# Bias of similarities in a cross-attention kernel: from six small TensorE passes to one VectorE multiply-and-sum with a broadcast load

## The chip, the cores and the metric

One Trainium2 chip, one core of it. The metric is the device time of one execution in microseconds (us); the kernel before takes 112.34 us, the median of three runs (112.3 to 112.38).

## What is computed

A block of three parts acts on x, 128 rows of 256 (L = 128, D = 256): a cross attention to a context of S = 12544 rows of 256, a self attention and a feed-forward part. The change touches the first one alone. Cut to what matters (h is x after layer normalisation, c the context):

```
w1, w2, w3 = w_sim[:d], w_sim[d:2*d], w_sim[2*d:]
Sim = (h @ w1)[:, :, None] + (c @ w2)[:, None, :] + einsum('bid,bjd->bij', h * w3, c) + b_sim[0]
A = softmax(Sim, axis=2)
hq_hat = A @ c
Batt = softmax(max(Sim, axis=2), axis=1)
hc_bar = Batt @ h
feats = concatenate([h, hq_hat, h * hq_hat, h * hc_bar])
x = x + feats @ W_qv + b_qv
```

The term h @ w1 + b_sim is one number for each of the 128 rows. It falls out of A, which a shift of a whole row does not change, and is needed only for Batt, that is for the row maximum of Sim. The kernel calls it hw1.

## The kernel before, in words

The context is cut into 25 chunks of 512 rows, 0 to 24; the last has 256. It is read twice from DRAM: transposed as "keys", for the scores, and as "rows", for the sum weighted by A. Every chunk of either kind is one load of 512 KB into one of ten slots of the ring `raw`. Both kinds go through one queue, SyncE's (SP): x first, then the keys 0 to 24, then the rows 0 to 24. `wait_for_slot` holds an item until the item ten places before it has been used. Into the keys two loads of 512 KB of the weights are mixed, behind keys 12 and 18 (`W_BEHIND`). The small vector `vec` and the scalar `bias` are loaded by ScalarE's queue at the start.

Phase of keys. TensorE multiplies a chunk in one of two ways. The "native" chunks 0, 4, 8, 16 and 24 are multiplied as they are (L925). The others are split into a high and a low part: ScalarE copies the high part (`keys_high`, L488), VectorE subtracts it from the chunk to get the low part (`keys_low`, L698), and TensorE does three products, L940 and L944 on the high part and L954 on the low. In chunks 10, 12, 14, 18, 20 and 22 (`SHARED`) GpSimd takes 448 of the 1024 columns of the low part (L454), so VectorE's piece has 576. For every two chunks VectorE empties two PSUM banks into `neg_scores` and takes the running minimum of the negated scores in `neg_max` (`running_max`, L721). VectorE's order is written out by hand: behind chunk k goes the low part of k + 2, and behind every odd k the running maximum of the pair. ScalarE also sums and centres weight blocks between its copies (L528, L539), the first four of them from the load behind key 12 and the next four from that behind key 18.

Turn of the phases. TensorE transposes the exponentials of chunks 0 and 1 (`turn`, L968), does the last native chunk between them, and multiplies them with their rows (`mix_early`, L979). `mix_early(0)` waits until the maximum of chunks 22 and 23 has been taken, because it writes into a PSUM bank that held scores:

```
                if k == 0:
                    pe.wait_ge(max_done, eviction_of[22] + 2)
```

Phase of rows. For chunks 2 to 24 TensorE transposes the exponentials of chunk k + 2 (L968) and does the products of chunk k (`mix`, L997 and L999). VectorE makes the low parts of rows and of transposed exponentials (L698, L728), ScalarE and GpSimd the high parts.

hw1 before. Behind the scores of chunk 1 TensorE does two products of `normed_t` with a column of `vec` (L1045) and one of a row of ones with `bias` (L1047) into column 0 of `mixed_ps`. A product of 32-bit numbers at full precision is several passes in the profile, so these are six rows of the trace. At the turn VectorE subtracts the last `neg_max` from it into `sim_max` (L766). Since `mix` overwrites `mixed_ps`, TensorE waits for `sim_max_done` ahead of the phase of rows. In chunk 3 `sim_max` is spread over the columns (L1060), and Batt follows from it.

## Time and profile before

| | |
|---|---|
| time, median of 3 runs | 112.34 us (112.3 to 112.38) |
| the profiled execution's own time | 112.1 us |
| its span, first to last instruction | 110.3 us |
| granted TensorE clock | 1.0 over the whole span |
| busy: TensorE, VectorE, ScalarE, GpSimd | 95%, 84%, 75%, 27% |
| moved by DMA | 29.82 MB |

The span leaves out 1.8 us of the execution's time that lie around it. A busy share is an average over phases: it does not say which engine holds the others at a given place. The rows that do follow further down.

### The profile page before, as it was taken

How to read it: one execution, taken by the hardware profiler on the slowest of the kernel's cores; microseconds unless marked ns; L12 is line 12 of the kernel's file. 1: busy time of each engine (PE TensorE's matmuls, PEld its weight loads, DVE VectorE, ACT ScalarE, POOL GpSimd, SP SyncE). 2: the span in 40 equal slices, each digit the busy share in tenths (PEclk: the TensorE clock that was granted, in tenths of full speed). 3: DMA queues.
4: the chain of work that ended last, by engine and by line, in shares of the span. 5: the costliest groups of instructions: out<-in, count | busy, mean ns of one | idle time of the engine just before them, and what ended most of it. 6: DMA issues, size and time to landing. Idle time of an engine off the chain costs nothing.

```text
span 110.3 us, 1855 instructions
## 1 busy us (share of the span) xinstructions
PE 105.1 (95%) x582; PEld 86.4 (78%) x583; DVE 93.1 (84%) x152; ACT 82.4 (75%) x171; POOL 29.3 (27%) x47
## 2 busy tenths in 40 slices
PE   5999999999999999999999999999999998998890
PEld 2368768588858888899899999989898997887680
DVE  1478999999998998999999999999999847674352
ACT  5067668899979989999999899988976725903450
POOL 2239200444043314233242424286330000200100
PEclk9999999999999999999999999999999999999999
DMA  2999999999999999999999999960000000000001
GB/s 72 367 406 423 416 422 422 416 422 422 409 420 417 418 415 423 417 420 442 442 389 423 415 422 425 406 260 0 3 0 0 0 6 0 0 0 0 6 3 48
DMA packets 8220, 29.82 MB, mean 270 GB/s; under 512 B 1042, under 2 KB 1298, under 8 KB 8082
## 3 DMA queue, kind: packets, MB, share of 16 engines
q1 hardware_dynamic: 8064, 29.69, 66.3%
q8 instruction: 5, 0.08, 0.3%
q14 instruction: 5, 0.04, 0.1%
q10 hardware_dynamic: 146, 0.01, 0.1%
HBM read 29.57 MB, written 0.13 MB: 269 GB/s over the span
## 4 chain that ended last, share of the span: by engine, by line
PE 94%; DVE 1%; issue 1%; ACT 1%; DVEq 0%; ACTq 0%
PE mixed_ps L997 18%; PE scores_ps L968 10%; PE mixed_ps L999 9%; PE scores_ps L940 8%; PE scores_ps L944 8%; PE scores_ps L954 8%; PE scores_ps L925 7%; PE scores_ps L910 4%; PE scores_ps L979 3%; PE scores_ps L1090 2%; PE mixed_ps L1142 2%; PE side_ps L1016 1%; PE scores_ps L1155 1%; PE side_ps L1133 1%; PE scores_ps L1016 1%; PE scores_ps L1125 1%
## 5 line engine op out<-in xcount | busy, mean ns | idle before, releaser
L698 DVE TENSOR_TENSOR pair<-raw,pair 128x1024 fp32r<-128x1024 f32 (+2 forms) x42 | 49.0, 1183 | 1.3 <-ACT pair L488 1.0
L488 ACT ACTIVATE pair<-raw 128x512 fp32r<-128x512 f32 (+1 forms) x42 | 34.5, 820 | 3.8 <-DMA raw<-keys_dram 3.4
L997 PE MATMUL mixed_ps<-pair,turned_high 128*128 128x512 f32 x84 | 32.3, 418 | 0.0
L999 PE MATMUL mixed_ps<-pair,turned_low 128*128 128x256 f32 x84 | 23.6, 281 | 0.0
L463 POOL CAST pair<-raw 128x512 fp32r<-128x512 f32 x22 | 13.6, 619 | 27.3 <-DVE pair L698 23.1
L997 PEld LDWEIGHTS mixed_ps<-pair,turned_high 128*128 128x128 f32 x84 | 15.8, 188 | 2.8
L520 ACT ACTIVATE turned_high<-scores_ps 128x512 fp32r<-128x512 f32 (+1 forms) x23 | 13.4, 584 | 4.0 <-PE scores_ps L968 4.0
L721 DVE TENSOR_SCALAR_CACHE_REDUCE neg_scores<-scores_ps,neg_max 128x1024 f32<-128x1024 f32 (+1 forms) x13 | 15.8, 1216 | 0.2
L999 PEld LDWEIGHTS mixed_ps<-pair,turned_low 128*128 128x128 f32 x84 | 16.0, 190 | 0.0
L728 DVE TENSOR_TENSOR turned_low<-scores_ps,turned_high 128x512 fp32r<-128x512 f32 (+1 forms) x23 | 15.3, 667 | 0.2 <-ACT turned_high L520 0.2
L968 PE MATMUL scores_ps<-ident,neg_scores 128*128 128x128 f32 x98 | 14.6, 272 | 0.0
L940 PE MATMUL scores_ps<-pair,q_high 128*128 128x512 f32 x40 | 14.1, 434 | 0.0
L507 ACT ACTIVATE neg_scores<-neg_scores,neg_max 128x1024 f32<-128x1024 f32 (+2 forms) x14 | 13.7, 977 | 0.0
L968 PEld LDWEIGHTS scores_ps<-ident,neg_scores 128*128 128x128 f32 x98 | 11.7, 140 | 1.4
L944 PE MATMUL scores_ps<-pair,q_low 128*128 128x512 f32 x40 | 12.5, 393 | 0.0
L954 PE MATMUL scores_ps<-pair,q_high 128*128 128x512 f32 x40 | 12.4, 391 | 0.0
L454 POOL TENSOR_TENSOR pair<-raw,pair 128x448 fp32r<-128x448 f32 x6 | 6.9, 1154 | 20.5 <-DVE pair L698 20.5
L940 PEld LDWEIGHTS scores_ps<-pair,q_high 128*128 128x128 f32 x40 | 7.5, 188 | 3.1 <-issue 1.9
L954 PEld LDWEIGHTS scores_ps<-pair,q_high 128*128 128x128 f32 x40 | 7.5, 188 | 1.7
L944 PEld LDWEIGHTS scores_ps<-pair,q_low 128*128 128x128 f32 x40 | 7.5, 188 | 1.6
L925 PE MATMUL scores_ps<-raw,q_t 128*128 128x512 f32 (+1 forms) x20 | 8.6, 553 | 0.0
L430 POOL TENSOR_TENSOR ln_rstd<-ln_var,minus_half 128x1 f32<-128x1 f32 x3 | 1.7, 555 | 21.8 <-DVE ln_var L842 12.7
(189 smaller groups left out, 130.6 us busy)
## 6 DMA issues: line engine op xcount, KB each, us to landing
raw<-keys_dram SPq DMA_DIRECT2D x24, 512.0 KB, 10.0
raw<-rows_dram SPq DMA_DIRECT2D x24, 512.0 KB, 9.2
w<-weights_dram SPq DMA_DIRECT2D x1, 1792.0 KB, 9.9
w<-weights_dram SPq DMA_DIRECT2D x2, 512.0 KB, 10.4
const<-const_dram SPq DMA_DIRECT2D x1, 832.0 KB, 11.5
raw<-keys_last_dram SPq DMA_DIRECT2D x1, 256.0 KB, 10.2
raw<-rows_last_dram SPq DMA_DIRECT2D x1, 256.0 KB, 6.8
x_sb<-x_dram SPq DMA_DIRECT2D x1, 128.0 KB, 2.2
```

The costliest lines, as they stand in the source:

```text
L488: nc.scalar.activation(pair[:, use % PAIR_BUFS, 0, 0:columns], raw[:, slot(item), 0:columns], ACT.Copy)\
L507: nc.scalar.activation(neg_scores[:, first:last], neg_scores[:, first:last], ACT.Exp, bias=neg_max[:, EVICTIONS:EVICTIONS + 1], scale=-1.0 ...
L698: nc.vector.tensor_tensor(out=pair[:, use % PAIR_BUFS, 1, 0:columns], in0=raw[:, slot(item), 0:columns], in1=pair[:, use % PAIR_BUFS, 0, 0 ...
L721: nc.vector.tensor_scalar(neg_scores[:, first_col:last_col], scores_ps[:, first // 2 % 3, scores_at:scores_at + last_col - first_col], -1. ...
L728: nc.vector.tensor_tensor(out=turned_low[:, k % TURNED_BUFS, 0:width_of(k)], in0=probs_turned_ps[k % TURNED_BUFS][:, 0:width_of(k)], in1=t ...
L925: last = nc.tensor.matmul(out_ps, q_t[:, a, :], keys_part(raw[:, slot(k), :], k, a), start=(a == 0), stop=(a == DH - 1))
L940: nc.tensor.matmul(out_ps, q_high[:, a, :], keys_part(high, k, a), start=(a == 0), stop=False)
L944: nc.tensor.matmul(out_ps, q_low[:, a, :], keys_part(high, k, a), start=False, stop=False)
L954: last = nc.tensor.matmul(out_ps, q_high[:, a, :], keys_part(low, k, a), start=False, stop=(a == DH - 1))
L968: last = nc.tensor.transpose(probs_turned_ps[k % TURNED_BUFS][:, t * P:(t + 1) * P], neg_scores[:, col:col + P], ident[:, :])
L997: nc.tensor.matmul(mixed_ps[:, :].rearrange("p (h d) -> p h d", h=2), probs_high, both[:, :, t * D:(t + 1) * D], start=(k == EARLY and t = ...
L999: last = nc.tensor.matmul(mixed_ps[:, 0:D], probs_low, rows_tile(high, t), start=False, stop=(k == LATE - 1 and end))
```

## The change

The two halves of hw1 change engine. The array `bias` in DRAM becomes one row of 257 numbers, w1 and behind it the scalar b_sim. SyncE's queue loads it behind key 14 and repeats it over all 128 partitions by reading the same row 128 times, into `w1_rows`. VectorE multiplies `normed` with it and sums along the row in one instruction, placed ahead of the low part of chunk 19. The subtraction at the turn takes the sum and the scalar from SBUF. TensorE's products of hw1 go, with ScalarE's load of `bias`, and its wait for `sim_max_done` moves from the start of the phase of rows to chunk 3, in front of the product that reads `sim_max`.

```
-        bias = sb("bias", [1, 1])
+        w1_rows = sb("w1_rows", [P, D + 1])
+        hw1_parts = sb("hw1_parts", [P, D])
+        hw1_sum = sb("hw1_sum", [P, 1])
...
+                if k == 14:
+                    sp.dma_start(w1_rows[:, :], bias_in.to_broadcast([P, D + 1])).then_inc(w1_rows_loaded, 16)
...
-            act.dma_start(bias[:, :], bias_in).then_inc(bias_loaded, 16)
...
             for e, chunks in enumerate(evictions):
                 for k in chunks:
+                    if k + 2 == 19:
+                        dve.wait_ge(w1_rows_loaded, 16)
+                        dve.wait_ge(normed_done, DH)
+                        nc.vector.scalar_tensor_tensor(hw1_parts[:, :], normed[:, :], 1.0, w1_rows[:, 0:D], ALU.mult,
+                                                       ALU.mult, accum_out=hw1_sum[:, :]).then_inc(hw1_done, 1)
                     if k + 2 < CHUNKS and not is_native(k + 2):
                         keys_low(k + 2)
                 running_max(e)
...
-            nc.vector.tensor_tensor(out=sim_max[:, :], in0=hw1_ps, in1=neg_max[:, EVICTIONS:EVICTIONS + 1],
-                                    op=ALU.subtract).then_inc(sim_max_done, 1)
+            nc.vector.scalar_tensor_tensor(sim_max[:, :], hw1_sum[:, :], w1_rows[:, D:D + 1],
+                                           neg_max[:, EVICTIONS:EVICTIONS + 1], ALU.add, ALU.subtract)\
+                .then_inc(sim_max_done, 1)
...
-                if k == 1:
-                    pe.wait_ge(ones_set, 1)
-                    pe.wait_ge(vec_loaded, 16)
-                    pe.wait_ge(bias_loaded, 16)
-                    pe.wait_ge(normed_t_done, DH)
-                    for a in range(DH):
-                        nc.tensor.matmul(hw1_ps, normed_t[:, a, :], vec[:, VC_W1 + a:VC_W1 + a + 1],
-                                         start=(a == 0), stop=False)
-                    nc.tensor.matmul(hw1_ps, ones[0:1, :], bias[0:1, 0:1],
-                                     start=False, stop=True).then_inc(hw1_done, 1)
...
-            pe.wait_ge(sim_max_done, 1)
             for k in range(EARLY, CHUNKS):
                 if k + 2 < CHUNKS:
                     turn(k + 2)
                 if k == EARLY + 1:
+                    pe.wait_ge(sim_max_done, 1)
...
-        "bias": a["L0_xattn_b_sim"].reshape(1, 1),
+        "bias": np.concatenate([a["L0_xattn_w_sim"][0:D], a["L0_xattn_b_sim"].reshape(1)]).reshape(1, D + 1),
```

SyncE's queue around key 14, before (in the kernel before, line 401 loads keys and line 404 weights; ten keys and x go ahead):

```order
L401 DMA raw<-keys_dram 128x1024 [waits low_done] x2
L404 DMA w<-weights_dram 128x1024
L401 DMA raw<-keys_dram 128x1024 [waits low_done]
L401 DMA raw<-keys_dram 128x1024 [waits native_done]
L401 DMA raw<-keys_dram 128x1024 [waits low_done] x3
L401 DMA raw<-keys_dram 128x1024 [waits native_done]
L404 DMA w<-weights_dram 128x1024
```

The same stretch with the change; the names are those that the listing gives, so `w_rows` is `w1_rows`:

```order
L402 DMA raw<-keys_dram 128x1024 [waits low_done] x2
L405 DMA w<-weights_dram 128x1024
L402 DMA raw<-keys_dram 128x1024 [waits low_done]
L402 DMA raw<-keys_dram 128x1024 [waits native_done]
L408 DMA w_rows<-bias_dram 128x257
L402 DMA raw<-keys_dram 128x1024 [waits low_done] x3
L402 DMA raw<-keys_dram 128x1024 [waits native_done]
L405 DMA w<-weights_dram 128x1024
```

The new load stands behind key 14, ahead of keys 15 to 24, of the second load of weights and of all rows.

VectorE from the running maximum of chunks 14 and 15 to that of 18 and 19, before (576 columns is the low part of chunk 18, the 1024 behind it that of chunk 19):

```order
L721 TENSOR_SCALAR neg_scores,neg_max<-scores_ps,neg_max 128x1024 [waits max_done,pair_used]
L698 TENSOR_TENSOR pair<-raw,pair 128x576 [waits high_done]
L698 TENSOR_TENSOR pair<-raw,pair 128x1024 [waits high_done]
L721 TENSOR_SCALAR neg_scores,neg_max<-scores_ps,neg_max 128x1024 [waits max_done,pair_used]
L698 TENSOR_TENSOR pair<-raw,pair 128x576 [waits high_done]
```

And with the change:

```order
L723 TENSOR_SCALAR neg_scores,neg_max<-scores_ps,neg_max 128x1024 [waits max_done,pair_used]
L700 TENSOR_TENSOR pair<-raw,pair 128x576 [waits high_done]
L765 SCALAR_TENSOR_TENSOR hw_parts,hw_sum<-normed,w_rows 128x256 [waits normed_done,w1_rows_loaded]
L700 TENSOR_TENSOR pair<-raw,pair 128x1024 [waits high_done]
L723 TENSOR_SCALAR neg_scores,neg_max<-scores_ps,neg_max 128x1024 [waits max_done,pair_used]
```

One instruction has come between the low parts of chunks 18 and 19; the others keep their order.

## Rows read from the trace of the kernel before

**Rows 1.** The page: busy time by engine, and the chain that ended last by engine.

```profile
PE 105.1 (95%) x582; PEld 86.4 (78%) x583; DVE 93.1 (84%) x152; ACT 82.4 (75%) x171; POOL 29.3 (27%) x47
...
PE 94%; DVE 1%; issue 1%; ACT 1%; DVEq 0%; ACTq 0%
```

**Rows 2.** The chain in order of time, 8 to 12 us: start us, us, what.

```profile
9.77 0.34 PE mixed_ps L1045 x4
10.11 0.31 PE mixed_ps L1047 x2
10.42 0.66 PE scores_ps L940 x2
...
11.99 0.46 PE scores_ps L940 x2
```

**Rows 3.** VectorE by time, phase of keys: start us, us, [idle before <-releaser].

```profile
9.18 2.36 DVE L698 TENSOR_TENSOR pair<-raw,pair 128x1024 fp32r<-128x1024 f32 x2 [0.50 <-ACT pair L488]
...
32.33 0.75 DVE L698 TENSOR_TENSOR pair<-raw,pair 128x576 fp32r<-128x576 f32 x1
33.55 1.22 DVE L698 TENSOR_TENSOR pair<-raw,pair 128x1024 fp32r<-128x1024 f32 x1 [0.47 <-ACT pair L488]
...
38.92 0.75 DVE L698 TENSOR_TENSOR pair<-raw,pair 128x576 fp32r<-128x576 f32 x1
...
41.93 0.08 DVE L721 DVE_READ_ACCUMULATOR neg_scores<-scores_ps,neg_max 128x1 f32 x1
42.13 1.28 DVE L721 TENSOR_SCALAR_CACHE_REDUCE neg_scores<-scores_ps,neg_max 128x1024 f32<-128x1024 f32 x1
43.34 0.08 DVE L721 DVE_READ_ACCUMULATOR neg_scores<-scores_ps,neg_max 128x1 f32 x1
43.54 0.48 DVE L721 TENSOR_SCALAR_CACHE_REDUCE neg_scores<-scores_ps,neg_max 128x256 f32<-128x256 f32 x1
```

**Rows 4.** TensorE by time: the low part of chunk 22, and the first product of `mix_early(0)`.

```profile
39.88 0.40 PE L954 MATMUL scores_ps<-pair,q_high 128*128 128x512 f32 x1
...
43.54 0.45 PE L979 MATMUL scores_ps<-raw,turned_early 128*128 128x256 f32 x1
```

**Rows 5.** The chain in order of time at the turn.

```profile
43.63 1.88 PE scores_ps L979 x8
...
45.94 1.73 PE scores_ps L979 x8
```

**Rows 6.** ScalarE by time, from the load of weights behind key 18 to key 20.

```profile
31.23 0.42 ACT L528 ACTIVATE w_sum_out<-w 128x256 f32<-128x256 f32 x1 [0.46 <-DMA w<-weights_dram]
...
32.45 1.06 ACT L488 ACTIVATE pair<-raw 128x1024 fp32r<-128x1024 f32 x1
33.68 1.06 ACT L488 ACTIVATE pair<-raw 128x1024 fp32r<-128x1024 f32 x1 [0.17 <-DMA raw<-keys_dram]
```

**Rows 7.** ScalarE by time: keys 11 and 12, and the weights behind key 12.

```profile
19.14 1.06 ACT L488 ACTIVATE pair<-raw 128x1024 fp32r<-128x1024 f32 x1 [0.15 <-DMA raw<-keys_dram]
20.44 1.06 ACT L488 ACTIVATE pair<-raw 128x1024 fp32r<-128x1024 f32 x1 [0.24 <-DMA raw<-keys_dram]
21.69 0.42 ACT L528 ACTIVATE w_sum_out<-w 128x256 f32<-128x256 f32 x1 [0.19 <-DMA w<-weights_dram]
```

**Rows 8.** Busy time by stretch; behind the engines: granted clock, DMA share, GB/s.

```profile
30.00:35.00 5.00, 5.00 (x20) 3.47 (x19) 4.53 (x8) 4.17 (x10) 1.26 (x2) 1.00 1.03 420
...
108.90:110.30 1.40, 0.00 (x0) 0.00 (x0) 0.00 (x0) 0.00 (x0) 0.00 (x0) 1.00 0.27 94
```

**Rows 9.** VectorE's groups by form, 90 us to the end: shapes xcount | busy us, mean ns.

```profile
L862 DVE SCALAR_TENSOR_TENSOR neg_scores<-scores_ps,ln_rstd,const 128x256 f32<-128x256 f32 x1 | 0.5, 476 | 0.0
```

**Rows 10.** VectorE by time in the first chunks of rows.

```profile
46.98 0.68 DVE L728 TENSOR_TENSOR turned_low<-scores_ps,turned_high 128x512 fp32r<-128x512 f32 x1
```

**Rows 11.** The start of the first product of `mix(2)` in TensorE's timeline.

```profile
48.30 0.48 PE L997 MATMUL mixed_ps<-pair,turned_high 128*128 128x512 f32 x1
```

More of the change, by code:

```diff
@@ L213, in build @@
         batt_ps = banks[5]
-        hw1_ps = mixed_ps[:, 0:1]
         b_mean_ps = banks[4][:, 0:D]
@@ L237, in build @@
         vec_loaded = sem("vec_loaded")
-        bias_loaded = sem("bias_loaded")
+        w1_rows_loaded = sem("w1_rows_loaded")
         w_qv_loaded = [sem(f"w_qv_loaded{n}") for n in range(2)]
```

## The prediction

> **What bounds the kernel now.** I read the page first. TensorE is busy 95% of the span and makes up 94% of the chain that ended last [rows 1], and the list of waits names none of its matmuls between the first warming ones and the projections behind the phase of rows. Read so, TensorE is the bound, and whatever it stops doing is gained. Since a matmul's busy time is modelled and overlaps its neighbour's, I then looked for places at which TensorE starts something just when another engine has finished.
>
> The chain in order of time shows the removed work [rows 2]: L1045 takes 0.34 us and L1047 0.31 us, and the pair of L940 behind them 0.66 us where the next pair takes 0.46 us.
>
> VectorE's timeline is the second view. From 9.18 us to 44 us VectorE stands idle for over 0.2 us only once: 0.47 us ahead of the low part of chunk 19, released by ScalarE [rows 3]. Around it the rows touch, low parts and running maxima in turn, none released by TensorE. So in the phase of keys VectorE runs by its own clock, and TensorE rides behind it. How near: the low part of chunk 22 is ready at 38.92 + 0.75 = 39.67 us, and TensorE starts on it at 39.88 us, 0.21 us later [rows 3, 4]. At the turn nothing is left. The maximum of chunks 22 and 23 ends at 43.34 + 0.08 = 43.42 us; 0.12 us later, at 43.54 us, VectorE starts its next maximum, which waits for that one, and in the same hundredth TensorE starts `mix_early(0)`, which waits for the same semaphore [rows 3, 4]. The gap of 0.12 us is that of a wait just released: VectorE shows it also between 42.01 and 42.13 us [rows 3]. And this `mix_early` takes 1.88 us in the chain where the other takes 1.73 us [rows 5]: the difference is time in which TensorE was held. **So the time of the turn, 43.54 us, is set by VectorE**, and the phase of rows follows from it without a stop.
>
> What sets VectorE's chain is the third view. Behind the idle 0.47 us it is continuous to the turn, so it hangs on its start at 33.55 us. The high part of chunk 19 ended at 32.45 + 1.06 = 33.51 us; ScalarE began it behind two weight sums, the first of which waited 0.46 us for the load of weights behind key 18 and started at 31.23 us; key 20 was waited for as well [rows 6]. So DMA holds ScalarE, ScalarE holds VectorE, VectorE holds TensorE. And DMA has no room: its sixteen engines are busy throughout the stretch around it (share 1.03), at 420 GB/s [rows 8].
>
> **The change part by part.**
>
> 1. *TensorE's six passes go*, by 0.34 + 0.31 = 0.65 us, and with the pair behind them by up to 0.85 us [rows 2]. This comes off at 9.8 us, ahead of a stretch in which TensorE follows VectorE. By the low part of chunk 22 at most 0.21 - 0.12 = 0.09 us of it can be left, and at the turn none, since TensorE is held there now. Bounds for the gain: 0 and 0.85 us; I take **0**, by the rows at the turn, which lie on the path. The gain becomes waiting ahead of low parts between chunks 19 and 23.
>
> 2. *The new load* moves 128 x 257 x 4 = 131,584 bytes behind key 14. The trace has no load of such a kind in the full stretch. The nearest row is the store of the output, 128 rows of 1 KB: in 108.90 to 110.30 us the share is 0.27 of sixteen engines, so 0.27 x 1.4 = **0.38 us** of all of them [rows 8]. From below, by bytes alone at the full stretch's rate: 131.6 KB / 420 GB/s = 0.31 us. From above I take twice the row's price, 0.76 us, for 128 reads of one and the same row in DRAM, which no row shows. I take 0.38. Since the engines are full, everything behind it in the queue lands that much later: keys 15 to 24, the weights behind key 18, the rows.
>
> The DMA page of the Trainium skill ("DMA: Bandwidth & Descriptors", Anatomy of one DMA) would price a load at about 2.0 us fixed plus its bytes, here about 2.3 us by its fit, an estimate. The rows speak against counting the fixed part here: keys 11 and 12 and the weights behind them, 512 KB each, are taken up at 19.14, 20.44 and 21.69 us, 1.25 to 1.3 us apart [rows 7], which is their bytes alone (0.524 MB / 420 GB/s = 1.25 us).
>
> 3. *The wait chain with it.* Weights 31.23 + 0.38 = 31.61; high part of 19 from 32.83 to 33.89; low part of 19 at 33.93 instead of 33.55. Behind that VectorE's row of work is unbroken, so the maximum of 22 and 23 ends at 43.80 and `mix_early(0)` starts at 43.92 instead of 43.54: **+0.38 us**. TensorE is there in time: it gets the low part of chunk 22 at 39.67 + 0.38 + 0.12 = 40.17 us, 0.29 us later than now, and keeps that lag of 0.29 us, less than 0.38.
>
> 4. *VectorE's new instruction.* The nearest row is a multiply of the same kind and size, 0.476 us, which reads PSUM [rows 9]; with the accumulator's read, 0.08 us [rows 3], 0.56 us; without PSUM perhaps 0.1 less. Bounds 0.45 and 0.56. It starts when the low part of 18 is done, at 33.08 us, with its data long there (the load goes out six transfers ahead of key 20), and ends by 33.64 us. The low part of 19 can't start before 33.93. The cover is the idle time that ScalarE leaves, now 0.47 and then 0.85 us; if it were gone the price would be 0.56 us; by the old start at 33.55 it would be up to 0.09 us. I take **0**.
>
> 5. *`sim_max`* is one instruction of one column in either kernel, and its reader in chunk 3 comes 6 us later: 0. *The wait for it* moves from 47.5 us to chunk 3; `sim_max` is there at 44.3 us, so it ends nothing now: 0. *ScalarE's load of `bias`* is one tiny packet ahead of everything: 0.
>
> 6. *The phase of rows.* The first low part of exponentials is ready at 46.98 + 0.68 = 47.66 us and `mix(2)` starts at 48.30 us [rows 10, 11]. VectorE, DMA and TensorE all slip by 0.38 us, so this slack of 0.64 us stands. TensorE has no stop in the phase that could take the slip back.
>
> Sum: 0 + 0.38 + 0 + 0 = +0.38 us, on the profiled execution 112.1 + 0.38 = 112.5 us. The median of the runs before lies 0.24 us above that execution; on it the forecast is 112.34 + 0.38 = **112.7 us**. A measurement of this kernel can tell about 0.2% (0.22 us) from no change.
>
> **The rivals.**
>
> *Faster: TensorE keeps what it no longer does.* The place is the turn. If the 0.12 us ahead of `mix_early(0)` is what a change from L968 to L979 costs and no wait, the start can move forward, and 0.65 us are gained: 112.34 - 0.65 = 111.7 us. For it speaks the chain, TensorE to 94%, and that no wait of it is listed. Against it speak the other `mix_early`, which follows the same L968 and is 0.15 us shorter, and that VectorE's low part of chunk 22 allows 0.09 us at most. It decides only if the maxima end over 0.1 us before 43.42. Chance 0.1.
>
> *No change: the slip is swallowed ahead of chunk 19.* From the weights behind key 12 (21.69 us) to those behind key 18 (31.23 us) lie seven transfers of 1.25 us, 8.7 us, but 9.54 us passed: they came 0.8 us late by the queue's own pace [rows 6, 7]. Something disturbed one or more DMA engines in between. If that falls elsewhere once the instructions have moved, the high part of 19 is ready by 33.51 - 0.8 + 0.38 = 33.1 us, and VectorE's new instruction sets the start instead, at 33.55 to 33.64 us: 0 to +0.09 us, 112.3 to 112.4 us. Chance 0.2.
>
> *Slower, much: a load's fixed cost is paid in the queue*, the skill's 2 us or all 128 rows on few engines: by rows, one engine would take 16 x 0.38 = 6 us for the 128 rows, and the last of the keys' shares would come late by as much. 112.34 + 2.3 = 114.6 us by the one and 118.4 us by the other. Rows 7 speak against it. Chance 0.03.
>
> **How the numbers follow.** The forecast (DMA's slip reaches the turn, +0.31 to +0.76 us) has 0.67; its own range is 112.65 to 113.1 us. The range reaches down to the case of no change: 112.3 to 113.1 us, leaving out the faster rival, the dear load and a little besides. Faster by over 0.2%: 0.1. Within 0.2%: 0.2. Slower by over 0.2%: 0.67 + 0.03 = 0.7.
>
> **What would show it.** In the changed kernel: L1045 and L1047 gone and the chunks behind them starting 0.65 to 0.85 us earlier on TensorE up to chunk 18; small waits of TensorE for VectorE's low parts between 19 and 23; the weights behind key 18 taken up at 31.6 us; VectorE's new row of about 0.5 us from 33.1 us, and still an idle piece of some 0.3 us ahead of the low part of 19, released by ScalarE; the maxima ending at 43.8 us and L979 starting at 43.9 us. The forecast is wrong if L979 starts before 43.6 us, or if the weights are taken up at 31.2 us or earlier; part 2 is mis-sized if they come at 31.5 or 32.0 us.

## The result, and the profile after

| | before | after |
|---|---|---|
| median of the runs | 112.32 us (6 runs, 111.8 to 112.38) | 114.28 us (6 runs, 113.73 to 115.0) |
| ratio, 95% interval | 1 | 1.0195 (1.0162 to 1.0228) |
| the profiled execution's own time | 112.1 us | 114.09 us |
| its span | 110.3 us | 112.3 us |

The kernel is 2% slower. The forecast was +0.38 us with a range up to 113.1 us; what came is about +2 us. The sign was right and the size was wrong by a factor of five.

In most of the kernels a few executions are longer, many of them at a mean granted clock of 0.985 instead of 1.0: the ratios leave these out, the medians below don't, and the trace of after_at256 (115.65 us) is of such a one.

The page of the changed kernel: its span, the busy times, the chain by engine, and the group of high parts.

```profile
span 112.3 us, 1845 instructions
PE 106.1 (94%) x577; PEld 84.5 (75%) x577; DVE 94.4 (84%) x154; ACT 82.6 (74%) x171; POOL 28.0 (25%) x47
...
PE 65%; DMA 15%; ACT 7%; DVE 4%; issue 4%; SPq 1%; DVEq 0%; ACTq 0%
...
L490 ACT ACTIVATE pair<-raw 128x512 fp32r<-128x512 f32 (+1 forms) x42 | 34.5, 822 | 5.3 <-DMA raw<-keys_dram 5.3
```

Beside [rows 1]: the six passes are gone (582 matmuls became 577 in the records, in which some can be missing), but DMA has appeared in the chain, with 15%, where TensorE alone had 94%. ScalarE's high parts waited 3.4 us for keys before and wait 5.3 us now.

ScalarE's timeline around the new load. It goes out behind key 14, so that key 15 is the next transfer behind it. The rows are the first weights (behind key 12), the high parts of keys 15, the next weights (behind key 18), and the high parts of keys 19 and 20.

```profile
22.95 0.42 ACT L530 ACTIVATE w_sum_out<-w 128x256 f32<-128x256 f32 x1 [0.21 <-DMA w<-weights_dram]
...
27.47 1.06 ACT L490 ACTIVATE pair<-raw 128x1024 fp32r<-128x1024 f32 x1 [0.82 <-DMA raw<-keys_dram]
...
32.75 0.40 ACT L530 ACTIVATE w_sum_out<-w 128x256 f32<-128x256 f32 x1
...
33.87 1.06 ACT L490 ACTIVATE pair<-raw 128x1024 fp32r<-128x1024 f32 x1
...
35.41 1.06 ACT L490 ACTIVATE pair<-raw 128x1024 fp32r<-128x1024 f32 x1 [0.48 <-DMA raw<-keys_dram]
```

The weights behind key 18 are taken up at 32.75 us instead of 31.23 us [rows 6]: 1.52 us later, where 0.38 us was forecast. Before, ScalarE waited 0.46 us for them; here the row shows no wait. DMA holds ScalarE earlier, at key 15. The chain in order of time has it: from there ScalarE works without a stop to the high part of chunk 19.

```profile
15.95 11.49 DMA raw<-keys_dram
...
33.87 1.07 ACT pair L490
34.94 0.02 issue
34.96 0.03 DVE pair L700
```

But the lateness doesn't start at the load. The weights behind key 12, ahead of it in the queue, are taken up at 22.95 us instead of 21.69 us [rows 7], already 1.26 us late. Two things make that up. In this execution the first keys came late (the high part of key 2 starts at 8.86 us, in the trace of before at 8.09 us), and the transfers then follow one another more slowly:

```profile
19.11 1.06 ACT L490 ACTIVATE pair<-raw 128x1024 fp32r<-128x1024 f32 x1 [0.22 <-DMA raw<-keys_dram]
20.40 1.06 ACT L490 ACTIVATE pair<-raw 128x1024 fp32r<-128x1024 f32 x1 [0.23 <-DMA raw<-keys_dram]
21.67 1.06 ACT L490 ACTIVATE pair<-raw 128x1024 fp32r<-128x1024 f32 x1 [0.21 <-DMA raw<-keys_dram]
```

These are keys 10, 11 and 12 of the changed kernel. With the weights at 22.95 us the four are 3.84 us apart, 1.28 us each, where before it was 1.25 [rows 7]. The windows say the same; the stretch from 10 to 20 us lies wholly ahead of the new load. The columns are busy us of TensorE, its weight loads, VectorE, ScalarE and GpSimd with the counts, the granted clock, DMA's share, and GB/s. First before, then the changed kernel.

```profile
10.00:20.00 10.00, 10.00 (x40) 7.28 (x41) 9.94 (x13) 6.98 (x9) 1.67 (x3) 1.00 1.03 419
23.00:25.00 2.00, 2.00 (x10) 1.63 (x10) 2.00 (x4) 2.00 (x4) 1.09 (x1) 1.00 1.02 418
```

```profile
10.00:20.00 10.00, 9.88 (x37) 6.69 (x37) 9.81 (x12) 6.80 (x8) 0.00 (x0) 1.00 1.03 413
23.00:25.00 2.00, 2.00 (x11) 1.63 (x9) 2.00 (x4) 1.73 (x5) 1.07 (x1) 1.00 1.03 392
30.00:35.00 5.00, 5.00 (x20) 3.40 (x19) 4.68 (x9) 4.82 (x10) 1.16 (x1) 1.00 1.03 406
```

The share is 1.03 in both, the rate is 413 and 406 GB/s instead of 419 and 420 [rows 8]. The engines are as busy as before and move less. In the records of single packets the 4 KB packets of keys take 161.7 ns on average between 8 and 22 us, before they took 159.1 ns. So there are two questions: what the new load costs, and what slows all the others.

VectorE around the new instruction (L765) and at the turn, and TensorE's `mix_early(0)` (L987; L962 is the product with a low part):

```profile
33.48 0.88 DVE L700 TENSOR_TENSOR pair<-raw,pair 128x576 fp32r<-128x576 f32 x1
34.28 0.41 DVE L765 SCALAR_TENSOR_TENSOR hw_parts<-normed,w_rows 128x256 f32<-128x256 f32 x1
34.63 0.08 DVE L765 DVE_READ_ACCUMULATOR hw_parts<-normed,w_rows 128x1 f32 x1
34.96 1.23 DVE L700 TENSOR_TENSOR pair<-raw,pair 128x1024 fp32r<-128x1024 f32 x1 [0.26 <-ACT pair L490]
...
45.06 0.08 DVE L723 DVE_READ_ACCUMULATOR neg_scores<-scores_ps,neg_max 128x1 f32 x1
45.27 0.48 DVE L723 TENSOR_SCALAR_CACHE_REDUCE neg_scores<-scores_ps,neg_max 128x256 f32<-128x256 f32 x1
```

```profile
38.44 0.73 PE L962 MATMUL scores_ps<-pair,q_high 128*128 128x512 f32 x2 [0.55 <-DVE pair L700]
...
45.27 1.97 PE L987 MATMUL scores_ps<-raw,turned_early 128*128 128x256 f32 x8
```

The mechanism at the turn is the one that was argued from [rows 3, 4]. VectorE's maximum and `mix_early(0)` again start in the same hundredth, now at 45.27 us, 0.13 us after the maximum of chunks 22 and 23 has ended at 45.14 us. TensorE waits visibly for a low part, 0.55 us. The turn is 1.73 us later than before.

### The profile page after: what moved, and what is told of

The parts are those of the page before. It is cut to its first block, busy times and chain, and to the rows that moved or that the text cites. A ratio compares the mean times of both kernels' runs of the same rounds, so it can differ in the third digit from the quotient of the medians.

```text
span 112.3 us, 1845 instructions
## 1 busy us (share of the span) xinstructions
PE 106.1 (94%) x577; PEld 84.5 (75%) x577; DVE 94.4 (84%) x154; ACT 82.6 (74%) x171; POOL 28.0 (25%) x47
## 2 busy tenths in 40 slices
DMA packets 8362, 29.96 MB, mean 267 GB/s; under 512 B 1056, under 2 KB 1440, under 8 KB 8224
## 4 chain that ended last, share of the span: by engine, by line
PE 65%; DMA 15%; ACT 7%; DVE 4%; issue 4%; SPq 1%; DVEq 0%; ACTq 0%
PE mixed_ps L1005 18%; DMA raw<-keys_dram 15%; PE scores_ps L976 10%; PE mixed_ps L1007 9%; PE scores_ps L987 3%; PE scores_ps L962 3%; ACT pair L490 3%; PE scores_ps L933 2%; DVE pair L700 2%; PE scores_ps L1087 2%; PE scores_ps L952 2%; PE scores_ps L948 2%; PE mixed_ps L1139 1%; PE side_ps L1024 1%; DVE neg_scores L723 1%
## 5 line engine op out<-in xcount | busy, mean ns | idle before, releaser
L700 DVE TENSOR_TENSOR pair<-raw,pair 128x1024 fp32r<-128x1024 f32 (+2 forms) x42 | 49.9, 1202 | 1.3 <-ACT pair L490 0.8
L466 POOL CAST pair<-raw 128x512 fp32r<-128x512 f32 x22 | 14.3, 652 | 27.0 <-DVE pair L700 20.5
L948 PE MATMUL scores_ps<-pair,q_high 128*128 128x512 f32 x40 | 14.1, 430 | 0.2 <-ACT pair L555 0.2
L962 PE MATMUL scores_ps<-pair,q_high 128*128 128x512 f32 x40 | 13.0, 406 | 0.7 <-DVE pair L700 0.5
L948 PEld LDWEIGHTS scores_ps<-pair,q_high 128*128 128x128 f32 x40 | 7.4, 188 | 4.4 <-issue 2.5
L962 PEld LDWEIGHTS scores_ps<-pair,q_high 128*128 128x128 f32 x40 | 7.0, 188 | 4.1 <-DVE pair L700 2.9
```

The costliest lines, as they stand in the source:

```text
L466: nc.gpsimd.tensor_copy(out=pair[:, use % PAIR_BUFS, 0, 2 * D:4 * D], in_=raw[:, slot(item), 2 * D:4 * D])\
L700: nc.vector.tensor_tensor(out=pair[:, use % PAIR_BUFS, 1, 0:columns], in0=raw[:, slot(item), 0:columns], in1=pair[:, use % PAIR_BUFS, 0, 0 ...
L948: nc.tensor.matmul(out_ps, q_high[:, a, :], keys_part(high, k, a), start=(a == 0), stop=False)
L962: last = nc.tensor.matmul(out_ps, q_high[:, a, :], keys_part(low, k, a), start=False, stop=(a == DH - 1))
```

## The experiments

Each kernel was run beside the kernel before on the same chip. The theories that the first four were to tell apart: the load costs more than its bytes; the ring `raw`, which three new tiles ahead of it move to another place in SBUF, makes every load slower; and, as a rival that would pull the other way, that TensorE's missing passes are a gain which something else eats. The tiles' places are those of the built programs: `raw` starts at byte 48896 of each partition before, and at 50976 after.

**The ring moved and nothing else (before_pad32).**

```
         vec = sb("vec", [P, VC])
         bias = sb("bias", [1, 1])
+        pad = sb("pad", [P, 1])
         x_sb = sb("x_sb", [P, D])
```

The tile holds 4 bytes per partition and moves all that follows by 32: `raw` starts at byte 48928.

> The kernel before with one unused tile of 32 bytes per partition ahead of x_sb, so that the ring raw starts at byte 48928 of each partition instead of 48896: still a multiple of 32, no longer of 64, as in the changed kernel (50976). Theory 'place': in the changed kernel every 4 KB packet got slower (159 ns before, 163 ns on the mean after) since raw no longer lies on 64 bytes, and the keys come late by that; then this kernel alone is 1.2 to 1.6 us slower than before (113.5 to 113.9 us), keys about 1.28 us apart instead of 1.25. Theory 'load' (the new load itself costs the queue 1.7 us): no change, 112.3 us. Theory 'DRAM' (the longer bias array moves the arrays in DRAM): no change, 112.3 us.

Measured: 112.92 us against 112.3 us, ratio 1.009 (1.0054 to 1.0126). An unused tile makes the kernel 0.9% slower, about 1 us where 1.2 to 1.6 us were expected. Its windows show the rate of the changed kernel:

```profile
10.00:20.00 10.00, 10.00 (x40) 7.30 (x41) 9.87 (x13) 6.72 (x9) 0.00 (x0) 1.00 1.03 413
...
30.00:35.00 5.00, 5.00 (x20) 3.44 (x19) 4.48 (x7) 3.91 (x8) 1.16 (x1) 1.00 1.02 409
```

Its 4 KB packets take 162.0 ns between 8 and 22 us. That the engines read a moved ring more slowly doesn't show: up to 44 us a high part on ScalarE takes 1,057 ns on average against 1,056 ns before, a whole low part on VectorE 1,220 ns against 1,219 ns. The place of the ring is one part of the loss, and as far as the trace shows it acts through the loads.

**The changed kernel with the same tile (after_pad32).** `raw` starts at 51008, which is a multiple of 64.

> The changed kernel with one unused tile of 32 bytes per partition ahead of x_sb, so that raw starts at byte 51008, a multiple of 64 again. Theory 'place': what is left is the slip that was forecast, 112.3 + 0.4 = 112.7 us, weights behind key 18 taken up by ScalarE at 31.6 us. Theories 'load' and 'DRAM': as the changed kernel, about 114.3 us.

Measured: 114.58 us, ratio 1.0216 (1.0186 to 1.0245), packets 161.8 ns. A multiple of 64 doesn't help: the place is as bad as that of the changed kernel.

**TensorE's passes away and no load in their place (before_nohw1).** `sim_max` takes a column of x in place of hw1, so this kernel leaves out the part h @ w1 + b_sim of Batt.

```
-            act.dma_start(bias[:, :], bias_in).then_inc(bias_loaded, 16)
...
-            nc.vector.tensor_tensor(out=sim_max[:, :], in0=hw1_ps, in1=neg_max[:, EVICTIONS:EVICTIONS + 1],
+            nc.vector.tensor_tensor(out=sim_max[:, :], in0=x_sb[:, 0:1], in1=neg_max[:, EVICTIONS:EVICTIONS + 1],
...
-                        nc.tensor.matmul(hw1_ps, normed_t[:, a, :], vec[:, VC_W1 + a:VC_W1 + a + 1],
-                                         start=(a == 0), stop=False)
-                    nc.tensor.matmul(hw1_ps, ones[0:1, :], bias[0:1, 0:1],
-                                     start=False, stop=True).then_inc(hw1_done, 1)
```

> The kernel before without TensorE's six passes of hw1 and without the load of bias; sim_max takes a column of x in place of hw1, so the h @ w1 + b_sim part of Batt is left out. Tiles stay where they are. My step 1 (the gain of 0.65 to 0.85 us is gone by the turn): no change, 112.3 us, TensorE earlier up to chunk 19, and mix_early(0) starting at 43.5 us as before. Rival (TensorE keeps it): 111.6 us, mix_early(0) at 42.8 to 42.9 us.

Measured: 112.28 us, ratio 1.0026 (0.9996 to 1.0055). Nothing is gained, though 0.65 us of TensorE's work is gone. TensorE and VectorE of this kernel at the turn:

```profile
43.12 0.60 PE L966 MATMUL scores_ps<-ident,neg_scores 128*128 128x128 f32 x4
43.68 1.10 PE L977 MATMUL scores_ps<-raw,turned_early 128*128 128x256 f32 x4
```

```profile
43.49 0.08 DVE L720 DVE_READ_ACCUMULATOR neg_scores<-scores_ps,neg_max 128x1 f32 x1
43.69 0.48 DVE L720 TENSOR_SCALAR_CACHE_REDUCE neg_scores<-scores_ps,neg_max 128x256 f32<-128x256 f32 x1
```

`mix_early(0)` still starts 0.11 us after VectorE's maximum has ended, at 43.57 us. VectorE held TensorE at the turn before the change too.

What held VectorE is another matter. The idle 0.47 us ahead of the low part of chunk 19 [rows 3], on which the prediction hung its chain, isn't there in this trace: VectorE is done with the low part of chunk 18 at 33.66 us, the high part of 19 is ready at 33.67 us, and ScalarE did not stand for the weights. The two low parts are merged into one row, as they are where hardly any time lies between them:

```profile
32.90 2.02 DVE L697 TENSOR_TENSOR pair<-raw,pair 128x576 fp32r<-128x576 f32 x2
```

**The load alone (before_load).** The kernel before with the broadcast load behind key 14, into a tile behind all others, so that `raw` stays at 48896. TensorE's passes stay, with `bias` now read from the last column of the longer array; the loaded rows go unused, and SyncE waits for them ahead of the store of the output.

```
+        w1_rows = sb("w1_rows", [P, D + 1])
...
+                if k == 14:
+                    sp.dma_start(w1_rows[:, :], bias_in.to_broadcast([P, D + 1])).then_inc(w1_rows_loaded, 16)
...
-        "bias": a["L0_xattn_b_sim"].reshape(1, 1),
+        "bias": np.concatenate([a["L0_xattn_w_sim"][0:D], a["L0_xattn_b_sim"].reshape(1)]).reshape(1, D + 1),
```

> The kernel before plus the broadcast load of 128 x 257 numbers behind key 14 into a tile behind all others, which nothing reads; raw stays at byte 48896, and the bias array has the 257 columns of the changed kernel. My step 2: +0.38 us, 112.7 us, weights behind key 18 taken up at 31.6 instead of 31.2 us, mix_early(0) at 43.9 us. Theory 'load': +1.7 to +2 us, 114.2 us, the whole delay between keys 14 and 15. Theory 'DRAM': +1.5 to +2 us, with keys late from the start.

Measured: 113.46 us, ratio 1.0134 (1.0106 to 1.0162), some 1.5 us for 131.6 KB. Around the load the rate halves while the share stays at 1.03:

```profile
10.00:20.00 10.00, 10.00 (x39) 7.08 (x39) 9.88 (x13) 6.97 (x9) 1.61 (x3) 1.00 1.03 420
23.00:25.00 2.00, 2.00 (x10) 1.67 (x9) 2.00 (x4) 1.90 (x4) 0.89 (x1) 1.00 1.03 200
```

and ScalarE, which reads key 15 next, stands for 1.69 us:

```profile
27.05 1.06 ACT L494 ACTIVATE pair<-raw 128x1024 fp32r<-128x1024 f32 x1 [1.69 <-DMA raw<-keys_dram]
```

The 128 packets of 1,028 bytes take 154 ns on average, about as much as a packet of 4 KB, and single 4 KB packets beside them take up to 598 ns. The array in DRAM has the length of the changed kernel's, but ahead of the load the rate is 420 GB/s and the packets take 159.2 ns: the longer array slows nothing by itself.

**The changed kernel with the ring on a multiple of 256 (after_at256).** `pad = sb("pad", [P, 56])` ahead of `x_sb`: `raw` starts at 51200.

> The changed kernel with one unused tile of 224 bytes ahead of x_sb, so that raw starts at byte 51200, a multiple of 256 (before: 48896, a multiple of 256 too; changed kernel: 50976; the two kernels padded by 32 bytes: 48928 and 51008, neither one). Theory '256' (the pace of the keys' packets, 159 ns or 162 to 163 ns, goes by whether a slot of raw starts on a multiple of 256 bytes): packets 159 ns again, the keys 1.25 us apart, and the time that of the load alone, 113.4 to 113.6 us. Theory 'length' (what counts is that raw lies further up, or the bias array in DRAM, not its alignment): packets 163 ns and 114.3 to 114.6 us.

Measured: 113.86 us, ratio 1.0113 (1.0077 to 1.015, from four executions), packets 159.2 ns. With its place mended the changed kernel costs about what before_load costs (1.0134); the two intervals overlap.

**A control for the place (before_pad256).** The kernel before with `pad = sb("pad", [P, 64])`: the ring moves by 256 bytes, to 49152.

> The kernel before with one unused tile of 256 bytes ahead of x_sb: raw at 49152, a multiple of 256. Theory '256': packets 159 ns and no change, 112.3 us, where the pad of 32 bytes cost 0.6 us. Theory 'length': 163 ns and 112.9 us.

Measured: 112.31 us, ratio 0.9996 (0.997 to 1.0022), packets 159.6 ns, and a rate of 420 GB/s:

```profile
10.00:20.00 10.00, 10.00 (x43) 7.52 (x42) 9.94 (x12) 6.98 (x9) 0.00 (x0) 1.00 1.03 420
```

So it isn't the unused tile or the shift as such.

**Halfway between (before_pad128).** `pad = sb("pad", [P, 32])`: `raw` at 49024, a multiple of 128 and of 64.

> The kernel before with an unused tile of 128 bytes ahead of x_sb: raw at byte 49024, a multiple of 128 and not of 256. Theory '256' as it stands (a start that is no multiple of 256 costs): packets of 4096 bytes at 162 to 163 ns on the mean and about 112.9 us, as with 32 bytes. Rival (a multiple of 64 or 128 would do, and the changed kernel padded to a multiple of 64 was slow for another reason): 159 ns and 112.3 us.

Measured: 112.85 us, ratio 1.0046 (1.0021 to 1.0072), packets 161.5 ns between 8 and 22 us and 163.4 ns between 20 and 40 us. All four places tried that are no multiple of 256 (48928, 49024, 50976, 51008) give 161.5 to 162.0 ns between 8 and 22 us; the three that are (48896, 49152, 51200), with ten kernels, give 159.1 to 160.0 ns. The packets are as slow as in before_pad32, but the kernel loses 0.5% where that one lost 0.9%; the intervals overlap, so the price of the place is known only as 0.5 to 0.9%.

**The same bytes from 128 rows in DRAM (before_load_rows).** As before_load, but the array holds the row 128 times and the load reads each row once.

```
-                    sp.dma_start(w1_rows[:, :], bias_in.to_broadcast([P, D + 1])).then_inc(w1_rows_loaded, 16)
+                    sp.dma_start(w1_rows[:, :], bias_in).then_inc(w1_rows_loaded, 16)
...
-        "bias": np.concatenate([a["L0_xattn_w_sim"][0:D], a["L0_xattn_b_sim"].reshape(1)]).reshape(1, D + 1),
+        "bias": np.concatenate([a["L0_xattn_w_sim"][0:D], a["L0_xattn_b_sim"].reshape(1)]).reshape(1, D + 1).repeat(P, axis=0),
```

> The kernel before plus the same load of 128 x 257 numbers behind key 14, but from 128 equal rows that lie one behind another in DRAM, instead of one row read 128 times. Theory 'same row' (reads of one DRAM row by all sixteen engines queue up and hold the keys behind them): +0.38 us, 112.7 us, packets of 1028 bytes 47 ns, the rate in 23 to 25 us not below 350 GB/s; the load from one row cost 1.1 us. Theory 'small packets' (128 packets of 1028 bytes hold the queue wherever they come from): 113.4 us as before.

Measured: 112.88 us, ratio 1.0027 (0.9992 to 1.0062). The packets of 1,028 bytes take 47 ns instead of 154, the rate holds at 414 GB/s, and key 15 is waited for 0.42 us instead of 1.69 us:

```profile
23.00:25.00 2.00, 2.00 (x11) 1.63 (x10) 2.00 (x5) 1.86 (x6) 1.17 (x1) 1.00 1.04 414
```

```profile
26.07 1.06 ACT L494 ACTIVATE pair<-raw 128x1024 fp32r<-128x1024 f32 x1 [0.42 <-DMA raw<-keys_dram]
```

One row of DRAM read 128 times is what makes the load dear, not its bytes and not that it is a load.

Only a part of this cheap load's slip reaches the turn. The weights behind key 18 are taken up at 31.31 us with no wait for DMA, and the low parts of chunks 18 and 19 follow each other with 0.07 us between them. From the taking up of the weights behind key 12 to `mix_early(0)` pass 21.66 us (21.98 to 43.64 us); in before, 21.85 us; in before_nohw1 and before_pad256, which have neither the load nor the idle 0.47 us, 21.41 and 21.52 us. So beside the latter two 0.14 to 0.25 us of the 0.34 us show (in them is a wait of 0.54 us for a key, at 35.58 us), and beside before none.

**Both mended in the changed kernel (after_rows_at256).** 128 rows in DRAM and `raw` at 51200; all that moved from TensorE to VectorE stays moved.

> The changed kernel with both: raw at byte 51200 and the load from 128 rows in DRAM. If place and same row are the whole of the excess, what I forecast comes out: 112.3 + 0.38 = 112.7 us, weights behind key 18 taken up at 31.6 us, VectorE's new instruction inside ScalarE's wait, mix_early(0) at 43.9 us. If something else in the change costs time (the new VectorE instruction, other fetches), it is above 113 us.

Measured: 112.92 us, ratio 1.0044 (1.0013 to 1.0075), which is +0.5 us (0.15 to 0.84). This is the kernel that the prediction had priced, at +0.38 us. The number fits, but in the trace the signs do not: the weights behind key 18 are taken up at 31.29 us and not at 31.6, with no wait, and `mix_early(0)` starts at 44.69 us and not at 43.9. Its low part of chunk 19 starts straight behind the new instruction:

```profile
33.25 0.41 DVE L766 SCALAR_TENSOR_TENSOR hw_parts<-normed,w_rows 128x256 f32<-128x256 f32 x1
33.59 1.22 DVE L701 TENSOR_TENSOR pair<-raw,pair 128x1024 fp32r<-128x1024 f32 x1
```

The high part of 19 was ready at 32.30 + 1.06 = 33.36 us, so in this execution VectorE's new instruction and not DMA set that start, as in the rival of no change. The maximum of chunks 22 and 23 ends at 43.44 us, as before. This execution (113.33 us, above the median) lost its time behind it, where ScalarE waited for the first rows and TensorE for ScalarE:

```profile
43.43 0.63 ACT L491 ACTIVATE pair<-raw 128x512 fp32r<-128x512 f32 x1 [1.01 <-DMA raw<-rows_dram]
```

```profile
44.69 1.97 PE L988 MATMUL scores_ps<-raw,turned_early 128*128 128x256 f32 x8 [1.08 <-ACT turned_early L516]
```

**Is there a version that beats both?** By the turn VectorE is late, so GpSimd was given a part of three more low parts, with the passes (before_shared) and without them (nohw1_shared, with the edit of before_nohw1).

```
-SHARED = (10, 12, 14, 18, 20, 22)
+SHARED = (10, 12, 14, 18, 19, 20, 21, 22, 23)
```

> The kernel before with GpSimd taking 448 columns of the low parts of chunks 19, 21 and 23 too. VectorE then has 1.4 us less to do ahead of the turn. If TensorE with its six passes is only just behind VectorE there (0.07 us), the gain is 0 to 0.1 us: 112.2 to 112.3 us, and mix_early(0) starts at about 43.5 us.

Measured: 112.85 us, ratio 1.005 (1.0017 to 1.0082), slower and not faster, with `mix_early(0)` at 44.31 us.

> The same split with TensorE's six passes left out too (sim_max takes a column of x instead of hw1). If the passes were worth nothing in the first kernel without them because VectorE held the turn, they are worth 0.5 to 0.85 us now that VectorE does not: 111.5 to 111.8 us. If they are worth nothing for another reason: 112.2 us.

Measured: 112.56 us, ratio 1.0007 (0.9971 to 1.0044), so the expected gain isn't there either. Its premise, that VectorE no longer holds the turn, fails in the trace: the maximum ends at 43.32 us and `mix_early(0)` starts at 43.57 us. Between the two kernels with this sharing lies 0.4%, but their intervals overlap, so whether the passes are worth anything beside it stays open. Why the sharing loses shows in the group of VectorE's low parts with 576 columns (line, engine, operation, count; busy us and mean ns of one; idle before). Before, then before_shared:

```profile
L698 DVE TENSOR_TENSOR pair<-raw,pair 128x576 fp32r<-128x576 f32 x6 | 4.5, 754 | 0.0
```

```profile
L698 DVE TENSOR_TENSOR pair<-raw,pair 128x576 fp32r<-128x576 f32 x9 | 8.6, 976 | 0.5 <-ACT pair L488 0.5
```

One takes 976 ns on average instead of 754. Two of the nine, at 35.44 and 38.87 us, take 1.63 and 1.62 us, more than the 1.22 us of a whole low part of 1024 columns, and one takes 1.03 us; the other six take 0.74 to 0.76 us. The two long ones start some 0.15 us after a piece of GpSimd's; the one at 38.87 us, and the two pieces of GpSimd's around it (the second from 38.72 us):

```profile
38.87 1.62 DVE L698 TENSOR_TENSOR pair<-raw,pair 128x576 fp32r<-128x576 f32 x1
```

```profile
37.15 2.72 POOL L454 TENSOR_TENSOR pair<-raw,pair 128x448 fp32r<-128x448 f32 x2 [0.69 <-DVE pair L698]
```

Three low parts became some 0.47 us shorter each on VectorE, 1.4 us in all, and three pieces 0.28 to 0.87 us longer, 2.0 us in all. So what GpSimd takes off VectorE it takes back from VectorE's own pieces beside it. ScalarE also waits 1.38 us for a key here, taken up at 30.12 us, likely behind a fetch of instructions (the last section).

**The change with everything learned (best).** The two large new tiles stand behind all others and the small `hw1_sum` in the place of `bias` (`raw` at 48896), the load comes from 128 rows and behind the first rows, the instruction stands ahead of the maximum of chunks 22 and 23, and the sharing is the larger one.

```
+                if k == 0:
+                    sp.dma_start(w1_rows[:, :], bias_in).then_inc(w1_rows_loaded, 16)
...
+                if e == eviction_of[23]:
+                    dve.wait_ge(w1_rows_loaded, 16)
+                    dve.wait_ge(normed_done, DH)
+                    nc.vector.scalar_tensor_tensor(hw1_parts[:, :], normed[:, :], 1.0, w1_rows[:, 0:D], ALU.mult,
+                                                   ALU.mult, accum_out=hw1_sum[:, :]).then_inc(hw1_done, 1)
```

> The change with what the runs showed to hurt taken out: the new tiles behind all others (raw at byte 48896), the load from 128 rows in DRAM and behind the first block of rows instead of key 14, VectorE's instruction ahead of the maximum of chunks 22 and 23, and GpSimd's share of chunks 19, 21 and 23. Theory: TensorE's passes are gained and the load and the instruction lie beside a wait: 111.5 to 111.9 us. Rival: the load holds the first rows or the instruction holds the turn, 112.2 us or more.

Measured: 112.76 us, ratio 1.0023 (0.9992 to 1.0053). That is 1.7% faster than the change as made, and no measurable difference to the kernel before; the expected 111.5 to 111.9 us did not come. Both conditions of the rival show in the trace: ScalarE waits 0.50 us for rows ahead of 42.44 us, and VectorE's instruction, at 41.88 us, stands directly in front of the maximum, which starts at 42.38 us. No version found beats before.

The runs side by side; the last column but one is the average of 4 KB packets between 8 and 22 us. The last one is the time from the taking up of the weights behind key 12 to that of key 15, less three transfers at the kernel's own pace (1.25 or 1.28 us): what the new load took in the queue in the profiled execution.

| kernel | ratio (95%) | `raw` at byte | 4 KB packets | the load took |
|---|---|---|---|---|
| after | 1.0195 (1.0162 to 1.0228) | 50976 | 161.7 ns | 4.52 - 3.84 = 0.68 us |
| after_pad32 | 1.0216 (1.0186 to 1.0245) | 51008 | 161.8 ns | 4.96 - 3.84 = 1.12 us |
| after_at256 | 1.0113 (1.0077 to 1.015) | 51200 | 159.2 ns | 5.22 - 3.75 = 1.47 us |
| before_load | 1.0134 (1.0106 to 1.0162) | 48896 | 159.2 ns | 5.56 - 3.75 = 1.81 us |
| before_load_rows | 1.0027 (0.9992 to 1.0062) | 48896 | 160.0 ns | 4.09 - 3.75 = 0.34 us |
| after_rows_at256 | 1.0044 (1.0013 to 1.0075) | 51200 | 159.7 ns | 4.09 - 3.75 = 0.34 us |
| before_pad32 | 1.009 (1.0054 to 1.0126) | 48928 | 162.0 ns | no load |
| before_pad128 | 1.0046 (1.0021 to 1.0072) | 49024 | 161.5 ns | no load |
| before_pad256 | 0.9996 (0.997 to 1.0022) | 49152 | 159.6 ns | no load |

## Why the prediction was right in direction and wrong in size

The step that failed is the sum's second term, the price of the load, and beside it a term that the sum hadn't at all, the place of the ring. Taken out of the changed kernel one by one, they are 0.8% for the place (after beside after_at256), 0.7% for reading one row 128 times (after_at256 beside after_rows_at256), and 0.4% for all that is left, together 1.95%. Added to the kernel before, they come out alike: 0.5 to 0.9% for the place and 1.3% (1.1 to 1.6%) for the whole load. For what is left 0.3% was forecast.

- **What bounds the kernel: right for the turn, too sure for what lies in front of it.** VectorE sets the time of the turn: in the changed kernel the maximum and `mix_early(0)` start together at 45.27 us, and before_nohw1 shows the same at 43.68 us. That DMA and ScalarE set VectorE's time was read from one idle piece of 0.47 us. It is there in the traces of before and of the changed kernel (0.26 us); in before_nohw1, before_pad256 and before_load_rows ScalarE's high part of 19 is ready only 0.01 to 0.11 us after VectorE has done with 18, and ScalarE did not wait for the weights. There the engines run nearly level, and DMA holds neither at that place.
- **Part 1, TensorE's passes at 0: right.** before_nohw1 gives 1.0026 (0.9996 to 1.0055), where 0.65 us would be a ratio of 0.994. The page's 94% of the chain for TensorE was a poor guide: it is put together from modelled ends. The rival in which TensorE keeps the 0.65 us fell with this run.
- **Part 2, the load at 0.38 us, bounds 0.31 and 0.76: the term that was mis-sized.** From 128 rows it takes 0.34 us in the queue, so the row of the store was a good price for the bytes; the run is 0.3% slower, which isn't clear of noise. From one row read 128 times it takes 0.7 to 1.8 us in the profiled executions, and 1.5 us by the runs of before_load. The prediction named this as unknown ("which no row shows") and then took twice the known price as the upper end, from no row. An unknown mechanism deserved an end from something that could go wrong in it, such as all 128 reads one after another. The dear-load rival had such a price, 114.6 us, but from a fixed cost of any load. That is refuted: before_load_rows is a load of the same size with no such cost, and the figure's nearness to 114.28 us is chance. The Trainium skill, "DMA: Bandwidth & Descriptors", Anatomy of one DMA, gives the 2.0 us that the prediction took from it for loads issued by GpSimd. Here SyncE issues them, and no trace shows such a gap in the full queue.
- **What no part had: the three new tiles.** The diff declares `w1_rows`, `hw1_parts` and `hw1_sum` ahead of `x_sb` and `raw`, in place of `bias`. They move the ring by 2,080 bytes, off a multiple of 256, and every load of keys and rows is then 1.5% to 2.6% slower in a queue that is full until all rows are loaded. Costing a change part by part must include the declarations: the prediction had costed every instruction and no address. That is about 1 of the 2 us, and it would have been there without any load.
- **Part 3, the wait chain: right for a large slip, only in part for a small one.** In the changed kernel the lateness does pass from DMA through ScalarE and VectorE to the turn, with ScalarE held at key 15 and not at the weights. What it transmits is larger: the weights 1.52 us late, the turn 1.73 us, `mix(2)` at 50.03 instead of 48.30 us [rows 11] again 1.73 us, the span 2.0 us. Single executions differ in when the queue starts, so of the 1.73 us some 0.8 us may be this execution's own; the shares are taken from the ratios of the runs. With the load at the forecast's price the chain carries less: in before_load_rows 0.14 to 0.25 us where 0.38 was forecast, and in after_rows_at256 the time is lost behind VectorE's maxima. That +0.5 us came where +0.38 had been forecast is therefore no proof of the path, and in part luck.
- **Part 4, VectorE's instruction at 0: right in the changed kernel.** 0.41 us, and its accumulator's read ends 0.43 us after its start (34.71 - 34.28), just under the forecast's 0.45 to 0.56. The 0.1 us taken off there for reading no PSUM stood on no row; with 0.56 us by the rows and 0.43 us measured it is 0.13 us. Behind it 0.26 us of idle time is left, released by ScalarE; some 0.3 us had been named. With a cheap load the cover just fails, by 0.2 us or so (after_rows_at256).
- **Part 6: right.** The slack of 0.64 us in front of the phase of rows gave nothing back: `mix(2)` is as late as the turn.
- **The rival of no change** had more in it than its chance of 0.2 says. What makes the weights 0.8 us late in the trace of before does fall elsewhere in other executions (the last section tells what it is likely to be). Its mechanism, VectorE's new instruction setting the start, is seen in after_rows_at256, where the lateness fell at the turn instead. In the changed kernel it did not decide: the slip was too large.

What isn't settled: why one row of DRAM read many times is slow (the rows show long packets, not their cause), why it took 0.7 us in one execution and 1.8 us in another, how much of a small slip reaches the end on average, and whether the passes are worth up to 0.4% once VectorE has room. A load on another queue wasn't tried.

## What to carry to other kernels

Where a queue is full for most of a kernel, look at the address of every tile before looking at instructions: a new tile that stands ahead of a ring in the order of allocation can cost more than the work that it serves, so declare small new tiles last. A load that repeats one row over the partitions was dear by its reads and not by its bytes; put the copies into DRAM. Moving it out of the full stretch is the other way, which no run tried by itself. An idle piece in one trace can be that execution's own; look for it in a second one before hanging a chain on it. And an engine with 94% of the chain is not yet the bound: look for starts that fall in the same hundredth as another engine's, and take the suspected work away to see.

## What the runs showed of the hardware that was not expected

**The place in SBUF sets how long a 4 KB packet takes.** Between 8 and 22 us it is 159.1 to 160.0 ns on average at starts that are multiples of 256 bytes and 161.5 to 162.0 ns at others, between 10 and 20 us 159.0 to 159.1 and 161.4 to 162.1 ns. DMA's share is 1.02 to 1.03 in both, the rate 419 to 420 and 412 to 414 GB/s. The Trainium skill, "DMA: Bandwidth & Descriptors", How a descriptor splits into AXI transactions, says that a transaction must start on a 256-byte boundary, so a descriptor that starts off one begins at the boundary below, and the bytes fetched ahead of its start cost beats of 32 bytes. Counted so, 4,096 bytes at an offset of 32 are 129 beats instead of 128, 0.8% more, and at an offset of 128 they are 132, 3.1% more, estimates by the count of the Trainium skill. The runs agree in which places are bad, but not in the count: they show 1.5% to 2.6% more and no growth from an offset of 32 to one of 128 (162.0 and 161.5 ns). The Trainium skill speaks of reading there; that writing into SBUF is split in the same way is an inference from these runs.

**128 reads of one row of 1,028 bytes.** They took 129 to 154 ns each on average in three of the four kernels that do so and 57 ns in the fourth, the changed kernel's profiled execution; from 128 rows 47 ns. While they run, single 4 KB packets beside them are slow too where the small ones are (up to 598 ns in before_load and 645 ns in after_at256, against 214 ns in the changed kernel), and before_load moved 200 GB/s for 2 us where before moved 418. The mean rate by slices of 2.8 us shows the hole in before_load at the ninth:

```profile
GB/s 90 374 382 414 423 420 418 421 257 418 414 418 420 417 415 417 421 423 418 453 412 409 418 420 420 421 330 4 3 0 0 6 0 0 0 0 0 6 3 47
```

**Fetching instructions takes the same engines.** In each trace five packets of 16 KB of the queue for instructions take 0.88 to 1.4 us each. The first fell at 28.4 us in the trace of before and at 28.1 to 37.0 us in others, with before_load and before_load_rows, whose instructions are the same, at 28.1 and 33.2 us. A likely reading is that the share of the load on the DMA engine which fetches comes later by about as much, and the whole load with it. In twelve of the fourteen traces the first fetch falls between 28.05 and 33.94 us, and in ten of these ScalarE stands 0.4 to 1.9 us for DMA, with the wait ending 2.0 to 3.2 us behind the fetch. The 0.46 us for the weights in before [rows 6] are one of them. In before_nohw1 and before_pad256 no wait over 0.2 us follows. In the two traces with the first fetch at 36.85 and 37.02 us it is the first rows that are waited for, 0.50 and 1.01 us. It was read from the traces and not tested by a run of its own.

**VectorE with GpSimd beside it.** A subtraction of 576 columns takes 0.75 us where GpSimd is idle or nearly so, and took 1.62 and 1.63 us where it started beside a subtraction of GpSimd's in before_shared. GpSimd's 448 columns take 1.14 to 1.17 us, but 1.61 to 1.67 us where VectorE was at such a piece when they started. It looks as if the later one stood until the earlier was done: VectorE's piece of 38.87 us ends at 40.49 us, 0.62 us behind the end of GpSimd's at 39.87 us. Dividing more operations between the two made them slower together.
